# Gram products for two samples at a time in every tile of a DLRM tower, with the lookups and layers moved between the gram parts

## The chip, the cores and the metric

The kernel runs on one core of one Trainium2 chip. The metric is the device time of one execution in microseconds. All arithmetic is fp32, the lookup products are fp32r.

## What is computed

For 2048 samples, 32 embedding rows of 256 numbers are gathered from 32 tables. All 496 dot products between pairs of the 32 rows are taken, 16 context numbers are added, and three dense layers follow.

```
e = stack([tbl_f[ids[:, f]] for f in range(32)], axis=1)      # [2048, 32, 256]
dots = einsum('bnd,bmd->bnm', e, e)                            # per sample 32 x 32
z = dots[:, iu, ju]                                            # 496 pairs i < j
h = concatenate([z, dense_ctx], axis=1)                        # 512 features
h = maximum(h @ W_top1 + b_top1, 0)                            # 512
h = maximum(h @ W_top2 + b_top2, 0)                            # 256
y = h @ W_top3                                                 # 1
```

## The kernel before, in words

The samples are cut into 16 tiles of 128. Each engine has its own program, written out by hand, and the engines are tied by semaphores alone; nothing is reordered.

**Where rows come from.** Six of the 32 tables have 1000 rows and stay in SBUF. Their rows are looked up by TensorE (`look_up`, L326 to 342: a one-hot matrix made by VectorE in `make_one_hot` times the table, 32 matmuls for two tiles of samples at once, kept by ScalarE in `keep_looked_up`). Three lookups fall on each tile, two in tile 0. The other 26 fields are gathered by GpSimd with one indirect DMA per field and tile (`gather`, L288 to 297): 128 rows of 1 KB. Fields go in units of two, 13 units a tile, and there are 9 places (`PLACES`) for units that have landed; a gather waits until the unit nine before it has been turned (`turn_done`).

**Turning.** `turn` (L311 to 324) transposes a unit on TensorE, four transposes into one PSUM bank of a ring of `RING` = 4, and ScalarE or VectorE copies it into `turned` (`keep_turned`, L477 and L603); `ACT_UNITS` says which engine takes which unit. The copy of a tile's units must wait until the gram products of the tile before are done, since `turned` is a single buffer. Turn n waits for the copy of turn n - `RING`.

**Gram products.** `gram` (L344 to 362) goes over 32 groups in `PARTS` = 8 parts. In tiles 0 to 14 each sample has its own 32-column product, 128x32 weights and 31 moving columns, four samples side by side on four column tiles, into two banks (`gram_ps`). Each fp32 matmul stands in the trace twice, so one tile has 512 weight loads and 512 matmuls. The last tile alone uses `last_gram` (L364 to 380): two samples share the weights (64 columns) and the moving operand (62 columns), 256 weight loads and 256 matmuls, into four banks (`quad_ps`). Half of what they compute is between different samples and not used; ScalarE and VectorE first move the used blocks of the second samples to where `unfold` reads them (`align`).

**After the gram.** VectorE transposes the blocks of 32 (`unfold`), ScalarE picks the 496 pairs (`pick`), TensorE turns the features (`turn_features`), ScalarE keeps them, then come `layer1` (four parts, 32 matmuls in the trace), `keep_hidden1` on ScalarE, `layer2` (8 matmuls in the trace) and `last_layers` on VectorE.

**TensorE's order** around the change, for a tile t from 1 to 14: `turn_all` (the units of t not yet turned, the features of tile t - 1 after unit 6, then all of layer 1 of tile t - 1), and then eight times a slice of the tile's lookups (10 or 11 matmuls) and a gram part; layer 2 of t - 1 behind part 0; one unit of tile t + 1 is turned behind each of parts 3 to 6 (`EARLY_AFTER`), and a last slice of the lookups stands behind part 7.

ScalarE in tile t: three copies, the last lookup's copy, the pick, a copy, the features, a copy, `place` (the looked up rows into `turned`, two activations), two copies, `keep_hidden1`, then the lookups' copies. VectorE: `unfold`, six copies, then the one-hots with `last_layers` behind the first.

Of the kernel before, what the change touches and what calls it, by code (L numbers as in the profile page):

```python
# [38 lines left out]
def dlrm_tower(nc, dense_ctx, ids, small_ids, tables, w1, b1, w2, b2, w3, out):  # L39
# [30 lines left out]
    ACT_UNITS = [0, 1, 2, 6, 8, 10, 12]  # L70
    RING = 4
# [5 lines left out]
    EARLY_AFTER = [3, 4, 5, 6]  # L77

    TURN_FEATURES_AFTER = 6
    PARTS = 8  # L80
    GPP = GROUPS // PARTS
    BANK_GROUPS = GROUPS // 2
# [3 lines left out]
    LAST_BANKS = 4  # L86
    LAST_GROUPS = GROUPS // LAST_BANKS

# [22 lines left out]
    with ctx:  # L111
# [16 lines left out]
        with nc.sbuf_tensor("landed", [SP, SMALL, SUB, 2, D], fp32) as landed:  # L128
# [29 lines left out]
        last_h2 = turn_ps[2]  # L158
# [8 lines left out]
                   for bank in (gram_ps[:, 1, :], top_ps)]  # L167
# [24 lines left out]
        gram_done = sem("gram_done")  # L192

        last_gram_done = sem("last_gram_done")
# [115 lines left out]
        def _(pe):  # L310
# [33 lines left out]
            def gram(t, portion):  # L344
# [6 lines left out]
                if t == 0 and portion == PARTS // 2:  # L351
# [12 lines left out]
            def last_gram(portion):  # L364
                t = TILES - 1
                if portion == 0:
                    pe.wait_ge(act_kept, n_act_kept(BEGIN[t + 1] - 1))
                    pe.wait_ge(dve_kept, n_dve_kept(BEGIN[t + 1] - 1))
                    pe.wait_ge(placed, 2 * t + 1)
                    pe.wait_ge(unfolded, t)  # L370
                for g in range(portion * GPP, (portion + 1) * GPP):
                    at = g % LAST_GROUPS * WIDE
                    for c in range(CHUNKS):
                        for h in range(HALVES):
                            s = QUADS * g + 2 * h
                            pair = turned[:, c, s:s + 2, :]
                            last = pe.matmul(quad_ps[h * 2 * FIELDS:(h + 1) * 2 * FIELDS, g // LAST_GROUPS, at:at + WIDE],  # L377
                                             pair.rearrange("d s f -> d (s f)"), pair[:, :, 0:COLS], start=(c == 0), stop=(c == CHUNKS - 1))
                if (portion + 1) * GPP % LAST_GROUPS == 0:
                    last.then_inc(last_gram_done, 1)  # L380
# [48 lines left out]
            def turn_all(t):  # L429
# [5 lines left out]
                for m in range(M1):  # L435
                    layer1(t - 1, m)

            def look_between(t, k):

                made = FIRST[t + 1] - FIRST[t]  # L440
                for n in range(made):
                    begin, end = (n * (PARTS + 1) + made - 1) // made, ((n + 1) * (PARTS + 1) + made - 1) // made
                    if begin <= k < end:
                        look_up(FIRST[t] + n, PRODUCTS * (k - begin) // (end - begin),
                                PRODUCTS * (k + 1 - begin) // (end - begin))
# [291 lines left out]
```

## Time and profile before

| | |
|---|---|
| median of 3 runs | 896.95 us (895.36 to 898.39) |
| the profiled execution's own time | 892.55 us |
| its span in the profile | 890.7 us |
| TensorE matmul busy | 601.0 us (67%) |
| TensorE weight load busy | 524.1 us (59%) |
| VectorE busy | 225.9 us (25%) |
| ScalarE busy | 204.6 us (23%) |
| GpSimd busy | 398.0 us (45%) |
| mean granted TensorE clock | 0.85 |

A tile after the first takes 54.6 us. Busy shares are averages over stretches with different limits, so a tile is best read in stretches.

### The profile page before, as it was taken

Reading aid. Unit: us, or ns where it says so; the run is one execution under the profiler, and the core shown is the slowest. Engines: PE = TensorE matmul, PEld = TensorE weight load, DVE = VectorE, ACT = ScalarE, POOL = GpSimd, SP = SyncE. Lnnn points to the kernel's source line nnn. Section 1 sums busy time; section 2 is a strip of 40 time slices with the busy share of each in tenths; the row PEclk is TensorE's granted clock in tenths of the full one; section 3 lists DMA queues with packets and bytes.
Section 4 is the critical chain, followed back from the end, with each engine's and each line's share of the span. In section 5 each row is a group of like instructions: output and inputs, shape, how many; then the busy total and the mean of one; then the engine's idle time right before and its main releaser. Section 6 shows DMA issues by size and latency. Waiting matters only on the chain.

```text
span 890.7 us, 24184 instructions
## 1 busy us (share of the span) xinstructions
PE 601.0 (67%) x11019; PEld 524.1 (59%) x11019; DVE 225.9 (25%) x578; ACT 204.6 (23%) x369; POOL 398.0 (45%) x426
## 2 busy tenths in 40 slices
PE   3557668486684867748577584875848668486687
PEld 2456557375572756737467474765737657375586
DVE  3444313123130231402223032231312313123122
ACT  4252303103030030401313022130210303103042
POOL 7563625526255361543715347262462625526220
PEclk9688969698796987969789697896969969698799
DMA  9962312313122141321313224131231312313110
GB/s 220 243 204 68 99 42 77 94 44 102 43 78 83 50 107 38 83 73 56 108 37 87 63 57 118 32 96 49 70 105 39 101 41 76 88 41 90 43 38 2
DMA packets 37459, 70.97 MB, mean 80 GB/s; under 512 B 10382, under 2 KB 23438, under 8 KB 37358
## 3 DMA queue, kind: packets, MB, share of 16 engines
q0 software_dynamic: 20112, 54.95, 22.1%
q1 hardware_dynamic: 17246, 14.48, 7.0%
q8 instruction: 87, 1.43, 0.7%
q14 instruction: 14, 0.11, 0.0%
HBM read 69.39 MB, written 0.01 MB: 78 GB/s over the span
## 4 chain that ended last, share of the span: by engine, by line
PE 42%; another core or an unknown queue 30%; issue 13%; ACT 12%; DMA 1%; DVE 1%; POOL 1%; ACTq 0%; DVEq 0%
PE look_ps L338 18%; PE quad_ps L358 12%; PE top_ps L420 6%; ACT turned L501 4%; ACT turned L483 3%; PE turn_ps L322 3%; PE quad_ps L322 2%; ACT area L550 2%; ACT ahead L490 1%; DMA rows<-in_tbl,row_ids 1%; PE quad_ps L377 1%; POOL rows L295 1%; PE top_ps L407 1%; ACT products L506 0%
## 5 line engine op out<-in xcount | busy, mean ns | idle before, releaser
L295 POOL DMA_INDIRECT rows<-in_tbl,row_ids x419 | 397.2, 948 | 458.1 <-PE turn_ps L322 184.1
L338 PE MATMUL look_ps<-one_hot,small 125*128 125x256 f32 (+1 forms) x1536 | 251.9, 303 | 104.7 <-issue 92.8
L338 PEld LDWEIGHTS look_ps<-one_hot,small 125*128 125x128 f32 x1536 | 214.0, 202 | 116.6 <-issue 112.3
L358 PE MATMUL quad_ps<-turned 128*32 128x31 f32 x7680 | 140.0, 204 | 121.8 <-issue 121.5
L358 PEld LDWEIGHTS quad_ps<-turned 128*32 128x32 f32 x7680 | 108.8, 115 | 166.9 <-issue 153.3
L674 DVE TENSOR_SCALAR one_hot<-ids_across,sub_row 125x256 fp32r<-125x256 int32 (+1 forms) x384 | 112.0, 364 | 145.8 <-PE look_ps L338 126.6
L322 PE MATMUL turn_ps<-ident,rows 128*128 128x128 f32 x424 | 64.5, 282 | 28.5 <-issue 14.7
L655 DVE TENSOR_TENSOR top_ps<-top_ps,b_sb 128x256 f32<-128x256 f32 x15 | 6.5, 433 | 299.8 <-PE top_ps L420 299.8
L490 ACT ACTIVATE ahead<-look_ps 128x512 f32<-128x512 f32 (+1 forms) x48 | 28.3, 590 | 232.5 <-PE look_ps L338 219.1
L407 PE MATMUL top_ps<-area,w_sb 128*128 128x128 f32 x488 | 61.9, 276 | 19.5 <-issue 18.8
L550 ACT ACTIVATE area<-top_ps,b_sb 128x128 f32<-128x128 f32 x61 | 17.5, 368 | 227.5 <-remote 225.2
L407 PEld LDWEIGHTS top_ps<-area,w_sb 128*128 128x128 f32 x488 | 57.8, 192 | 18.1 <-issue 17.2
L322 PEld LDWEIGHTS turn_ps<-ident,rows 128*128 128x128 f32 x424 | 48.2, 143 | 31.8 <-issue 28.2
L483 ACT ACTIVATE turned<-turn_ps 128x512 f32<-128x512 f32 x57 | 35.0, 631 | 114.2 <-PE quad_ps L358 76.2
L322 PE MATMUL quad_ps<-ident,rows 128*128 128x128 f32 x414 | 60.1, 279 | 0.8 <-DMA rows<-in_tbl,row_ids 0.8
L483 ACT ACTIVATE turned<-quad_ps 128x512 f32<-128x512 f32 x55 | 33.9, 631 | 90.6 <-PE quad_ps L358 70.8
L420 PE MATMUL top_ps<-w_sb,area 128*128 128x256 f32 x120 | 49.4, 585 | 4.1 <-ACT area L550 4.1
L618 DVE STREAM_TRANSPOSE products<-quad_ps 128x992 f32<-128x992 f32 x15 | 18.3, 1217 | 127.7 <-PE quad_ps L358 127.7
L322 PEld LDWEIGHTS quad_ps<-ident,rows 128*128 128x128 f32 x414 | 46.5, 142 | 2.9 <-DMA rows<-in_tbl,row_ids 1.2
L501 ACT ACTIVATE turned<-ahead 128x768 f32<-128x768 f32 x31 | 45.0, 1552 | 0.0
L420 PEld LDWEIGHTS top_ps<-w_sb,area 128*128 128x128 f32 x120 | 35.6, 311 | 13.9 <-ACT area L550 6.1
L609 DVE COPY turned<-quad_ps 128x512 f32<-128x512 f32 (+1 forms) x49 | 33.0, 681 | 34.1 <-PE quad_ps L322 14.6
(50 smaller groups left out, 169.9 us busy)
## 6 DMA issues: line engine op xcount, KB each, us to landing
rows<-in_tbl,row_ids POOLq DMA_INDIRECT x419
ids_across<-in_small_ids SPq DMA_DIRECT2D x45, 128.0 KB
landed<-in_tbl SPq DMA_DIRECT2D x6, 896.0 KB
w_sb<-in_W_top SPq DMA_DIRECT2D x4, 256.0 KB
landed<-in_tbl SPq DMA_DIRECT2D x6, 104.0 KB
w_sb<-in_W_top SPq DMA_DIRECT2D x1, 512.0 KB
area<-in_dense_ctx SPq DMA_DIRECT2D x16, 8.0 KB
row_ids<-in_ids SPq DMA_DIRECT2D x1, 240.0 KB
```

The source lines that it names most:

```text
L295: pool.indirect_dma_start(out=rows[:, n % PLACES, j, :], out_offset=None, in_=tables[f], in_offset=bass.IndirectOffsetOnAxis(ap=row_ids[:, ...
L322: last = pe.transpose(turn_ps[n % RING][:, at:at + P], rows[:, n % PLACES, j, c * P:(c + 1) * P], ident[:, :])
L338: last = pe.matmul(look_ps[:, c * width:(c + 1) * width], small[:, f, r, part, c * P:(c + 1) * P], one_hot[n % 2][:, r, 0:width], start=(r ...
L358: last = pe.matmul(gram_ps[q * FIELDS:(q + 1) * FIELDS, g // BANK_GROUPS, at:at + COLS], turned[:, c, s, :], turned[:, c, s, 0:COLS], star ...
L407: last = pe.matmul(bank[:, m * P:(m + 1) * P], w1_sb[:, c, m * P:(m + 1) * P], features_t[:, c, :], start=(c == 0), stop=(c == KC - 1))
L420: last = pe.matmul((last_h2 if t == TILES - 1 else top_ps)[:, 0:HIDDEN2], hidden1[:, c, :], w2_sb[:, c, :], start=(c == 0), stop=(c == M1 ...
L483: act.activation(turned[:, :, :, f:f + len(unit)], turn_ps[n % RING][:, 0:CHUNKS * len(unit) * P].rearrange("p (c f s) -> p c s f", c=CHUN ...
L490: act.activation(ahead[:, f, :, 0:tiles * P], look_ps[:, 0:CHUNKS * tiles * P].rearrange("p (c s) -> p c s", c=CHUNKS), ACT.Copy).then_inc ...
L501: act.activation(turned[:, :, :, fs].rearrange("p c s f -> p f c s"), ahead[:, fs, :, half * P:(half + 1) * P], ACT.Copy).then_inc(placed, 1)
L550: act.activation(hidden1[:, m, :], bank[:, m * P:(m + 1) * P], ACT.Relu, bias=b1_sb[:, m:m + 1]).then_inc(h1_kept, 1)
L609: dve.tensor_copy(turned[:, :, :, f:f + len(unit)], turn_ps[n % RING][:, 0:CHUNKS * len(unit) * P].rearrange("p (c f s) -> p c s f", c=CHU ...
L674: last = dve.tensor_scalar(one_hot[n % 2][:, r, 0:width], ids_across[0:SP, n % IDS_RING, 0:width], sub_row[:, r:r + 1], None, ALU.is_equal)
```

## The change

- `gram` takes the form that `last_gram` had, in all tiles: 16 wide products a part (32 weight loads and 32 matmuls a part in the trace, 256 a tile), into four banks of their own. The semaphore `gram_banks` counts banks, each after two parts.
- PSUM has eight banks, so the ring of turned units shrinks from 4 to 2. `ACT_UNITS` becomes every even unit.
- `align` runs in all tiles: ScalarE for banks 0 and 2, VectorE for banks 1 and 3, and `unfold` waits for all of it.
- Two units instead of four are turned early, behind parts 5 and 6.
- The lookups are no longer cut in slices: each of parts 0, 1 and 2 has one whole lookup (32 matmuls) in front, and none stands behind part 7.
- Layer 1 of the tile before leaves `turn_all` (except in the last tile); its four parts stand behind gram parts 2 to 5, and layer 2 behind part 6. ScalarE's `keep_hidden1` moves behind `align(t, 2)`, VectorE's `last_layers` behind the one-hots.
- The ids of every tile are laid out on the host in the order that only the last tile had.

```diff
-    ACT_UNITS = [0, 1, 2, 6, 8, 10, 12]
-    RING = 4
+    ACT_UNITS = [0, 2, 4, 6, 8, 10, 12]
+    RING = 2
-    EARLY_AFTER = [3, 4, 5, 6]
+    EARLY_AFTER = [5, 6]
+    LAYER1_BEHIND = 2
+    LAYER2_BEHIND = 6
...
-        quad_ps = psum("quad_ps", [P, LAST_BANKS, 512])
-        gram_ps = quad_ps[:, 0:2, :]
-        turn_ps = [psum(f"turn_ps{i}", [P, 512]) for i in range(RING - 2)] + [quad_ps[:, b, :] for b in (2, 3)]
+        gram_ps = psum("gram_ps", [P, GRAM_BANKS, 512])
+        turn_ps = [psum(f"turn_ps{i}", [P, 512]) for i in range(RING)]
...
                 for g in range(portion * GPP, (portion + 1) * GPP):
-                    at = g % BANK_GROUPS * COLS
-                    for c in range(CHUNKS):
-                        for q in range(QUADS):
-                            s = q * FIELDS + g
-                            last = pe.matmul(gram_ps[q * FIELDS:(q + 1) * FIELDS, g // BANK_GROUPS, at:at + COLS],
-                                             turned[:, c, s, :], turned[:, c, s, 0:COLS],
-                                             start=(c == 0), stop=(c == CHUNKS - 1))
-                if portion == PARTS - 1:
-                    last.then_inc(gram_done, 1)
+                    at = g % BANK_GROUPS * WIDE
                     for c in range(CHUNKS):
                         for h in range(HALVES):
                             s = QUADS * g + 2 * h
                             pair = turned[:, c, s:s + 2, :]
+                            last = pe.matmul(gram_ps[h * 2 * FIELDS:(h + 1) * 2 * FIELDS, g // BANK_GROUPS, at:at + WIDE],
+                                             pair.rearrange("d s f -> d (s f)"), pair[:, :, 0:COLS],
+                                             start=(c == 0), stop=(c == CHUNKS - 1))
+                if (portion + 1) * GPP % BANK_GROUPS == 0:
+                    last.then_inc(gram_banks, 1)
...
-                for m in range(M1):
-                    layer1(t - 1, m)
+                if t == TILES - 1:
+                    for m in range(M1):
+                        layer1(t - 1, m)
             def look_between(t, k):
+                if k < FIRST[t + 1] - FIRST[t]:
+                    look_up(FIRST[t] + k, 0, PRODUCTS)
...
                 for k in range(PARTS):
                     look_between(t, k)
-                    if t < TILES - 1:
-                        gram(t, k)
-                    else:
-                        last_gram(k)
-                    if t > 0 and k == 0:
+                    gram(t, k)
+                    if 0 < t < TILES - 1 and LAYER1_BEHIND <= k < LAYER1_BEHIND + M1:
+                        layer1(t - 1, k - LAYER1_BEHIND)
+                    if t > 0 and k == (0 if t == TILES - 1 else LAYER2_BEHIND):
                         layer2(t - 1)
                     if k in EARLY_AFTER and t + 1 < TILES:
                         turn(BEGIN[t + 1] + EARLY_AFTER.index(k))
-                look_between(t, PARTS)
...
             def unfold(t):
-                dve.wait_ge(gram_done, t + 1)
+                dve.wait_ge(act_aligned, 4 * (t + 1))
+                dve.wait_ge(dve_aligned, 4 * (t + 1))
```

## Rows read from the trace of the kernel before

**Rows 1.** The page's groups of instructions, GpSimd's gathers.

```profile
L295 POOL DMA_INDIRECT rows<-in_tbl,row_ids x419 | 397.2, 948 | 458.1 <-PE turn_ps L322 184.1
```

**Rows 2.** Busy time in five stretches of one tile (start:end, length, busy us, count).

```profile
core 0: us, PE busy (x) PEld busy (x) DVE busy (x) ACT busy (x) POOL busy (x), PEclk, DMA share, GB/s
422.68:431.38 8.70, 8.31 (x74) 8.00 (x73) 5.31 (x12) 7.69 (x14) 5.89 (x7) 1.00 0.33 93
431.38:449.01 17.63, 4.34 (x19) 3.08 (x18) 1.10 (x4) 0.03 (x1) 11.14 (x12) 0.63 0.38 104
449.01:453.34 4.33, 4.01 (x64) 3.32 (x64) 0.00 (x0) 1.14 (x4) 0.00 (x0) 0.52 0.01 4
453.34:460.98 7.64, 7.55 (x234) 6.96 (x233) 3.06 (x11) 0.60 (x1) 0.00 (x0) 1.00 0.03 8
460.98:477.26 16.28, 12.64 (x320) 11.06 (x320) 3.54 (x10) 1.75 (x4) 7.69 (x8) 1.00 0.28 73
```

**Rows 3.** Timeline of that tile, from the first gather in turn_all to layer 2.

```profile
423.66 0.94 POOL L295 DMA_INDIRECT rows<-in_tbl,row_ids  x1 [3.01 <-PE turn_ps L322]
...
444.93 0.95 POOL L295 DMA_INDIRECT rows<-in_tbl,row_ids  x1 [0.30 <-issue]
...
449.01 1.01 PE L358 MATMUL quad_ps<-turned 128*32 128x31 f32 x57 [1.19 <-issue]
...
449.14 1.14 ACT L550 ACTIVATE area<-top_ps,b_sb 128x128 f32<-128x128 f32 x4 [17.74 <-remote]
...
450.34 3.38 PE L420 MATMUL top_ps<-w_sb,area 128*128 128x256 f32 x8 [0.31 <-ACT area L550]
```

**Rows 4.** Groups of instructions on GpSimd between 423.6 and 449.0 us.

```profile
L295 POOL DMA_INDIRECT rows<-in_tbl,row_ids x18 | 17.0, 946 | 8.2 <-issue 5.2 <-PE turn_ps L322 3.0
```

**Rows 5.** Timeline around one pair of gathers behind an early turn.

```profile
460.98 0.95 POOL L295 DMA_INDIRECT rows<-in_tbl,row_ids  x1 [15.11 <-PE quad_ps L322]
...
461.95 0.58 PE L358 MATMUL quad_ps<-turned 128*32 128x31 f32 x43
...
463.72 0.37 PE L358 MATMUL quad_ps<-turned 128*32 128x31 f32 x16 [0.45 <-issue]
```

**Rows 6.** Timeline of gram parts and lookup slices with no gather about.

```profile
454.95 0.76 PE L358 MATMUL quad_ps<-turned 128*32 128x31 f32 x64
...
455.65 1.58 PE L338 MATMUL look_ps<-one_hot,small 125*128 125x256 f32 x11
...
457.15 0.76 PE L358 MATMUL quad_ps<-turned 128*32 128x31 f32 x64
```

**Rows 7.** Timeline of the last tile, which has no gathers left.

```profile
858.90 0.42 PEld L322 LDWEIGHTS turn_ps<-ident,rows 128*128 128x128 f32 x4
...
863.80 3.74 PE L407 MATMUL top_ps<-area,w_sb 128*128 128x128 f32 x32
...
867.47 1.15 PE L377 MATMUL quad_ps<-turned 128*64 128x62 f32 x32
...
868.77 1.99 PE L420 MATMUL top_ps<-w_sb,area 128*128 128x256 f32 x8 [0.15 <-ACT area L550]
...
870.70 6.75 PE L377 MATMUL quad_ps<-turned 128*64 128x62 f32 x224
```

**Rows 8.** Timeline of VectorE and ScalarE where a gram ends, in two tiles.

```profile
421.48 1.22 DVE L618 STREAM_TRANSPOSE products<-quad_ps 128x992 f32<-128x992 f32 x1 [7.66 <-PE quad_ps L358]
421.53 0.64 ACT L483 ACTIVATE turned<-turn_ps 128x512 f32<-128x512 f32 x1 [9.53 <-PE quad_ps L358]
...
871.89 0.72 ACT L522 ACTIVATE quad_ps<-quad_ps 32x248 f32<-32x248 f32 x2 [3.17 <-PE quad_ps L377]
...
877.49 0.89 DVE L626 COPY quad_ps<-quad_ps 32x248 f32<-32x248 f32 x2 [2.84 <-PE quad_ps L377]
```

**Rows 9.** Timeline near the start: a lookup, and a turn under gathers.

```profile
18.88 5.94 PE L338 MATMUL look_ps<-one_hot,small 125*128 125x256 f32 x32 [0.93 <-issue]
...
34.23 0.37 PE L322 MATMUL turn_ps<-ident,rows 128*128 128x128 f32 x1 [1.04 <-issue]
```

More of the change, by code:

```diff
@@ L157, in dlrm_tower @@
         last_h1 = [top_ps, look_ps, turn_ps[0], turn_ps[1]]
-        last_h2 = turn_ps[2]
+        last_h2 = gram_ps[:, 0, :]
         spare_ps = turn_ps[0]
@@ L166, in dlrm_tower @@
         high_ps = [bank[0:SP, 0:AT_ONCE * D].rearrange("p (r d) -> p r d", r=AT_ONCE)
-                   for bank in (gram_ps[:, 1, :], top_ps)]
+                   for bank in (gram_ps[:, GRAM_BANKS - 1, :], top_ps)]
         square = products[:, 0:COLS * ZROW].rearrange("p (i j) -> p i j", j=ZROW)
@@ L350, in gram @@
                         pe.wait_ge(unfolded, t)
[L351 removed]
+                if t == 0 and portion * GPP == GROUPS - BANK_GROUPS:
                     pe.wait_ge(low_parts, SMALL * STEPS)
                 for g in range(portion * GPP, (portion + 1) * GPP):
[L354 to L372 removed]
+                    at = g % BANK_GROUPS * WIDE
                     for c in range(CHUNKS):
@@ L376, in last_gram @@
                             pair = turned[:, c, s:s + 2, :]
[L377 to L380, printed above, removed]
+                            last = pe.matmul(gram_ps[h * 2 * FIELDS:(h + 1) * 2 * FIELDS, g // BANK_GROUPS, at:at + WIDE],
[3 more added lines that the diff above has]
+                    last.then_inc(gram_banks, 1)
             def turn_features(t):
@@ L514, in pick, with align @@
                 act.activation(features[:, CYCLIC:PAIRS], diagonal[:, 0:HALF, HALF], ACT.Copy).then_inc(picked, 1)
-            def align(b):
-                act.wait_ge(last_gram_done, b + 1)
-                both = quad_ps[:, b, 0:LAST_GROUPS * WIDE].rearrange("p (g h j) -> p h g j", h=2, j=COLS)
+            def align(t, b):
+                act.wait_ge(gram_banks, GRAM_BANKS * t + b + 1)
+                both = gram_ps[:, b, 0:BANK_GROUPS * WIDE].rearrange("p (g h j) -> p h g j", h=2, j=COLS)
                 for q in (1, 3):
@@ L577, in _ @@
                 if t > 0:
-                    for i in ACT_UNITS[:3]:
+                    for i in ACT_UNITS[:2]:
                         keep_turned(BEGIN[t] + i)
@@ L582, in _ @@
                         keep_looked_up(FIRST[t] - 1)
+                    keep_turned(BEGIN[t] + ACT_UNITS[2])
                     pick(t - 1)
@@ L589, in _ @@
                         keep_turned(BEGIN[t] + i)
-                    keep_hidden1(t - 1)
+                    if t == TILES - 1:
+                        keep_hidden1(t - 1)
                 for n in range(FIRST[t], FIRST[t + 1] - 1):
                     keep_looked_up(n)
-            align(0)
-            align(2)
+                align(t, 0)
+                align(t, 2)
+                if 0 < t < TILES - 1:
+                    keep_hidden1(t - 1)
             last_pick()
@@ L699, in _ @@
                 for k, n in enumerate(range(FIRST[t] + 1, FIRST[t + 1] + 1)):
+                    if n == FIRST[t + 1]:
+                        align(t, 1)
                     if n < len(LOOKUPS):
                         make_one_hot(n)
-                    if k == 0 and t > 0:
-                        last_layers(t - 1)
+                if t > 0:
+                    last_layers(t - 1)
                 if t == TILES - 1:
-                    last_layers(t - 1)
-            align(1)
-            align(3)
-            last_unfold()
+                    align(t, 1)
+                align(t, 3)
+            unfold(TILES - 1)
             last_pick()
```

38 lines of the change are left out of this document (12 added, 26 removed).

## The prediction

> **What bounds the kernel now.** The page comes first: no engine is busy all the time, TensorE least idle, GpSimd with its 419 gathers of 948 ns not the bound [rows 1]. So a tile has to be read in stretches [rows 2], the tile that starts at 422.68 and is followed by the next at 477.26, 54.58 us. TensorE is busy for 8.31 of 8.70 us while it turns units, then for 4.34 of 17.63 us, in which 19 matmuls start, then for nearly all of 12 us (4.33 and 7.64), and then for 12.64 of 16.28. The reader is to see that 13.3 us of idle time lie in one stretch. What it waits for there is told by the timeline [rows 3]: nothing that the profile shows ("issue"), and ScalarE, which needs the last matmul of layer 1, is let go at 449.14, at the moment at which TensorE runs again and 57 matmuls start in one microsecond. What else goes on is the gathers: the first at 423.66, the last issued at 444.93, 18 of them back to back [rows 3, 4]. 449.01 less 423.66 is 25.35 us, or **1.41 us a gather**, more than the 1.25 us at which GpSimd issues them. The same length stands around a pair of gathers behind an early turn: from 460.98 to 463.72 is 2.74 us, 1.37 a gather, and TensorE makes 43 matmuls in it and then stands [rows 5]. With no gather about it does not stand: gram part, slice and gram part follow each other at 454.95, 455.65 and 457.15 [rows 6]. And in the last tile, where no gathers are left, the gram starts at 867.47, 8.57 us after the first turn at 858.90 [rows 7], where the tile above took over 26. I read this as one cause: while gathers are being carried out, at about 1.4 us each, TensorE's matmuls complete only in a trickle, and it can run ahead of them by a limited count. Between 422.68 and 449.01, 26.3 us, 74 and 19 matmuls started, 93 in all [rows 2]. What fits into such a stretch is thus a number of matmuls, not an amount of time.
>
> **The change, part by part.** Durations are those of the profiled execution, 892.55 us, 4.40 us under the median of the runs.
>
> Gram. A narrow part of 64 matmuls takes 0.70 us (454.95 to 455.65), 10.9 ns each [rows 6], so 5.6 us a tile. The wide form takes 6.75 us for 224, 30.1 ns each [rows 7], so 7.7 us for 256. In TensorE's own time the change costs 2.1 us a tile, though it halves the instructions. A rule speaks for the change here: the Trainium skill (TensorE: Matmul & The Clock Gate, the section on 56 against 53.3 ns) says that starts of matmuls are never closer than some 25 ns however few the columns. By it the narrow gram would cost 12.8 us and the wide one save 5.1; the row shows less than half of that floor, and the sum goes by the row.
>
> Gathers and ring. A tile has 26 gathers either way. Before, 4 units were turned early, so 8 gathers ran beside gram parts, and 18 made the long stretch. Now 2 are turned early, so 4 gathers run beside parts and 11 units, **22 gathers**, follow in one stretch: 22 x 1.41 = 31.0 us, and with the 0.98 us from first turn to first gather (422.68 to 423.66) 32.0 us, against 26.3.
>
> What fills that stretch. Eleven turns come first. With a ring of 2 each turn waits for the copy of the turn two before, and so for its own kind's completion. How fast turns complete under gathers no row shows alone: the bounds are a turn per gather (1.41 us) and one per pair of gathers (2.8 us, then the gathers set the pace of the turns). I take 1.41, since in the first 8.70 us the turns and all of layer 1 started without a stop [rows 2]: 11 turns and the features, some 17 us. In the 15 us left stands the first lookup, 32 matmuls. The 93 matmuls that started in 26.3 us, scaled to 32.0, are 113; turns and features take 48, the lookup 32, and the other 33 are the first gram part, 32. The second lookup must wait for the first to complete and be copied, so it comes after the stretch.
>
> After the stretch. A slice of 11 lookups takes 1.50 us [rows 6], so a lookup of 32 takes 4.4. Second lookup 4.4, with 1.0 more for the lowered clock at its start: at 0.52 of the granted clock layer 2 took 3.38 us [rows 2, 3] and in the last tile 1.99 [rows 7], and a whole lookup near the start, at the lower of the two levels, 5.94 [rows 9]. A rest of part 0: 0.3. Gram part 1: 1.0. Third lookup 4.4. Parts 2 to 6: 4.8. Layer 1 in four parts: 3.7 [rows 7]. Two early turns: 0.9. Wait for `keep_hidden1` (1.14 us [rows 3], partly beside part 6): 0.5. Layer 2 at full clock: 2.0. Then the second early turn sends two gathers, and part 7's last semaphore completes only behind them: 3.0, of which the part's 1.0 is hidden. ScalarE's copy, now with no lookup slice in front of the next turn: 0.75 [rows 8]. The sum is 26.75, against 28.25 before (449.01 to 477.26). Gained in it are 11 of 85 lookup matmuls each 1.50 us that move forward (2.9), the stops beside four pairs of gathers (16.28 less 12.64 and what lies in them, some 4), and 1.4 of layer 2; lost are layer 1, wide parts and the waits.
>
> `align` (0.72 us on ScalarE, 0.89 on VectorE for a pair [rows 8]) is hidden for banks 0 to 2 by later parts. Bank 3 lies in front of `unfold` (1.22 us), so VectorE's first copy comes 0.9 us later; turns are paced by gathers there, which hides it, and without that cover it costs 0.9 a tile. One-hots have the wait for the third lookup's slot ahead of them, hidden by parts 1 and 2. `last_layers` and the dense load of SP have a whole turn phase to spare. The host's order of ids costs the chip nothing.
>
> A tile then takes 32.0 + 26.75 = 58.7 us, 4.1 more. Tiles 1 to 14 make 57. Last tile: the copies in a ring of 2 (0.43 turn, 0.64 copy and the ways between, about 0.8 a unit) and layer 1 still in `turn_all` bring the gram from 8.6 to about 13 us behind the first turn: 4.4. Start: a ring of 2 in 15 turns beside the splitting of tables, and the first gram wide: 2, between -1 and 6. Together 57 + 4.4 + 2 = 64 over 892.55 is 956.5, and with the 4.4 to the median **961, given as 960**.
>
> **The rivals.**
>
> A, turns go at the pace of a pair of gathers. Near the start single turns did start as far apart as the 34.23 row shows, alone after 1.04 us of idle time [rows 9]. Then nothing but turns fits into the stretch, and the first lookup and part 0 fall behind it: 5 us a tile more, 70 in all, about 1030. Against it: the table loads were under way there.
>
> B, the completions go on at turn speed through the whole stretch. Then the second lookup fits too: 5.4 us a tile less than the sum, 76 in all, about 885. For it: the first 8.70 us of the stretch in rows 2, with 74 matmuls. Against it: the rest of it, where 19 started in 17.63 us.
>
> C, on the other side, faster: the stall belongs to TensorE's own instructions and the gathers only go along with it. Its place is the 13.3 us of the long stretch and the 3.6 of the last one in rows 2. Of 711 matmuls a tile (74, 19, 64, 234 and 320) 256 go, so 0.64 are left, and of 16.9 us of idle time 6.1 go; the wide gram gives back 2.1, the copy and the alignment 0.9 more: 3.1 a tile gained, 43, and with the 6.4 of both ends 37 less: about 860. It decides if the stop ends earlier than 1.4 us times the gathers. For it: stops in rows 5 fall inside the dense narrow part, which is where instructions come fastest. Against it: rows 6 and 7 have the same density and no stop, and the stretch's length is the gathers' to some hundredths.
>
> D, a limit for each start of a matmul, whatever its columns, that rows 6 hide. If a narrow product cost what a wide one does, 30.1 ns [rows 7], the narrow gram would take 15.4 us and the wide one gain 7.7 where the sum loses 2.1: 9.8 a tile, 137 in all, about 825. Against it: 64 in 0.70 us. The Trainium skill's page named above has the milder form of this rule; by it the time would be about 860.
>
> E, the change does nothing: what TensorE gains and loses is all absorbed by the gathers' 26 x 1.41 = 37 us a tile. About 897.
>
> **Chances.** The forecast with its bounds (925 to 985) has 0.45, A 0.12, B 0.13, C 0.24, D 0.02, E 0.04. Differences under 0.3% can't be told from none. B is split, 0.08 faster, 0.02 the same and 0.03 slower. Faster: 0.34; the same: 0.06; slower: 0.60. Most of the chance is on two sides, so the likeliest case's own range is 925 to 985; the range given reaches to C's price and leaves out A: 855 to 1000.
>
> **What would show it.** Right: one long stretch of 22 gathers a tile and a stop that ends 31 us behind the first; one lookup and no more in it; no stop in the gram parts behind single pairs, except ahead of the next turns; wide parts of 0.96 us; about 450 matmuls a tile. Wrong: a stop that ends before 1.4 us times its gathers (C), two lookups inside it (B), or turns 2.5 us and more apart (A). The forecast falls if the stretch between two tiles' first turns is under 55 us.

## The result, and the profile after

The kernel after takes **984.99 us** (median of 4 runs, 981.01 to 989.16), the kernel before, measured beside it, 896.15 us (4 runs, 894.34 to 898.39). The ratio is 1.099 with a 95% interval of 1.093 to 1.105: slower, as forecast (960, range 855 to 1000), and 25 us above the forecast number. The profiled execution took 987.82 us with a span of 986.0. Executions of one kernel on one chip lie within 1.5% of each other, but for the kernel after on a chip of the experiments, where the profiled one took 698.84 us at a mean granted TensorE clock of 0.94 and the other 674.95 us at 0.97; the faster one is compared there.

The page of the kernel after, groups of instructions:

```profile
L294 POOL DMA_INDIRECT rows<-in_tbl,row_ids x419 | 397.2, 948 | 552.0 <-PE turn_ps L321 410.2
L321 PE MATMUL turn_ps<-ident,rows 128*128 128x128 f32 x838 | 167.1, 348 | 204.4 <-issue 76.8
L337 PE MATMUL look_ps<-one_hot,small 125*128 125x256 f32 (+1 forms) x1536 | 260.0, 336 | 63.0 <-issue 57.1
L358 PE MATMUL gram_ps<-turned 128*64 128x62 f32 x4096 | 166.5, 236 | 27.4 <-issue 25.1
```

The gathers are the same 419 of 948 ns [rows 1], and GpSimd waits 94 us longer between them: it is not the bound. The turns (the transposes of gathered rows on TensorE) now have 204.4 us of idle time in front of them. As before, the tile has to be read in stretches. Busy time of the kernel after in the two stretches of one tile, from its first turn to the end of the stop (the time in which TensorE hardly starts a matmul) and from there to the next tile's first turn:

```profile
core 0: us, PE busy (x) PEld busy (x) DVE busy (x) ACT busy (x) POOL busy (x), PEclk, DMA share, GB/s
457.75:490.39 32.64, 17.00 (x90) 14.21 (x90) 7.73 (x16) 8.63 (x14) 20.82 (x22) 0.71 0.35 96
490.39:518.90 28.51, 25.65 (x359) 23.81 (x360) 6.76 (x23) 4.32 (x11) 3.78 (x4) 0.92 0.09 26
```

The first stretch answers to the first two of [rows 2] and is 6.3 us longer, the second to the last three and is 0.3 us longer. This tile took 61.2 us; the first 13 of the 15 steps between the unfolds of neighbouring tiles have a mean of 60.2 (54.6 before). Inside the tile, TensorE and GpSimd in the timeline of the kernel after, with one of VectorE's copies:

```profile
459.11 0.94 POOL L294 DMA_INDIRECT rows<-in_tbl,row_ids  x1 [2.80 <-PE turn_ps L321]
...
466.99 0.63 PE L321 MATMUL turn_ps<-ident,rows 128*128 128x128 f32 x4 [1.61 <-DVE turned L590]
...
469.09 0.63 PE L321 MATMUL turn_ps<-ident,rows 128*128 128x128 f32 x4 [1.47 <-issue]
...
472.62 0.69 DVE L590 COPY turned<-turn_ps 128x512 f32<-128x512 f32 x1 [5.79 <-remote]
...
473.46 1.09 PE L321 MATMUL turn_ps<-ident,rows 128*128 128x128 f32 x4 [3.75 <-DVE turned L590]
...
477.64 1.09 PE L321 MATMUL turn_ps<-ident,rows 128*128 128x128 f32 x4 [3.09 <-issue]
...
478.38 4.64 PE L337 MATMUL look_ps<-one_hot,small 125*128 125x256 f32 x26
...
487.93 0.95 POOL L294 DMA_INDIRECT rows<-in_tbl,row_ids  x1 [0.30 <-issue]
...
490.39 1.54 PE L358 MATMUL gram_ps<-turned 128*64 128x62 f32 x23 [0.45 <-issue]
...
491.86 5.44 PE L337 MATMUL look_ps<-one_hot,small 125*128 125x256 f32 x32
...
498.32 4.09 PE L337 MATMUL look_ps<-one_hot,small 125*128 125x256 f32 x32
...
514.89 1.15 PE L358 MATMUL gram_ps<-turned 128*64 128x62 f32 x32
...
518.90 1.08 PE L321 MATMUL turn_ps<-ident,rows 128*128 128x128 f32 x4 [2.87 <-ACT turned L460]
```

From the first gather of the stretch (459.11) to the end of the stop (490.39) are 31.3 us for 22 gathers, 1.42 each (1.41 in [rows 3]). The last three turns start 4 us apart. That it is the completion of a matmul that comes late shows at the turn of 466.99: VectorE, idle for 5.79 us, begins its copy at 472.62 only, and the turn of 473.46 had to wait for that copy. One lookup and 9 matmuls of part 0 fit in, 23 of part 0 do not. At the end of the tile the next turn waits 2.87 us for ScalarE's copy. I read this as part 7's completion, held back by the pair of gathers of 515.23 and 516.48, which the copy has to wait for.

Two places outside the ordinary tile cost more. The last step but one between unfolds (tile 14) took 67.6 us against 54.0 in the kernel before. Its timeline in the kernel after:

```profile
917.02 1.98 PE L358 MATMUL gram_ps<-turned 128*64 128x62 f32 x32
918.92 7.09 PE L337 MATMUL look_ps<-one_hot,small 125*128 125x128 f32 x32
...
945.09 0.70 PE L321 MATMUL turn_ps<-ident,rows 128*128 128x128 f32 x4 [2.84 <-ACT turned L460]
...
961.17 1.15 PE L358 MATMUL gram_ps<-turned 128*64 128x62 f32 x32
```

Busy time and granted clock in that place of the kernel after:

```profile
917.00:925.00 8.00, 8.00 (x62) 7.87 (x61) 0.00 (x0) 1.08 (x3) 0.00 (x0) 0.50 0.00 0
```

The granted clock was 0.50, with TensorE busy for all 8 us: a part takes 1.98 us instead of 1.08, a lookup of half the columns 7.09. And the last tile needs 16.1 us from its first turn (945.09) to the gram (961.17), against 8.57 [rows 7]. The account of the 95.3 us between the two profiled executions (987.82 and 892.55), by the starts of the unfolds: 0.7 up to the first, 13 x 5.6 = 73, tile 14 13.6, last tile 6.1, end 1.6.

### The profile page after: what moved, and what is told of

It reads as the page before. It is cut to its first block and busy times, and to the rows that moved or that the text cites. A ratio compares the mean times of both kernels' runs of the same rounds, so it can differ in the third digit from the quotient of the medians.

```text
span 986.0 us, 16627 instructions
## 1 busy us (share of the span) xinstructions
PE 686.2 (70%) x7179; PEld 615.1 (62%) x7179; DVE 248.5 (25%) x638; ACT 229.9 (23%) x429; POOL 398.0 (40%) x426
## 5 line engine op out<-in xcount | busy, mean ns | idle before, releaser
L321 PE MATMUL turn_ps<-ident,rows 128*128 128x128 f32 x838 | 167.1, 348 | 204.4 <-issue 76.8
L337 PEld LDWEIGHTS look_ps<-one_hot,small 125*128 125x128 f32 x1536 | 246.1, 244 | 68.6 <-issue 66.6
L321 PEld LDWEIGHTS turn_ps<-ident,rows 128*128 128x128 f32 x838 | 126.0, 180 | 235.3 <-issue 232.5
L358 PE MATMUL gram_ps<-turned 128*64 128x62 f32 x4096 | 166.5, 236 | 27.4 <-issue 25.1
L358 PEld LDWEIGHTS gram_ps<-turned 128*64 128x64 f32 x4096 | 146.0, 148 | 51.7 <-issue 38.6
L460 ACT ACTIVATE turned<-turn_ps 128x512 f32<-128x512 f32 x112 | 68.6, 613 | 388.9 <-remote 261.8
L590 DVE COPY turned<-turn_ps 128x512 f32<-128x512 f32 x98 | 67.5, 688 | 259.5 <-remote 129.1
L608 DVE COPY gram_ps<-gram_ps 32x248 f32<-32x248 f32 x64 | 27.5, 430 | 240.3 <-PE gram_ps L358 200.0
L499 ACT ACTIVATE gram_ps<-gram_ps 32x248 f32<-32x248 f32 x64 | 22.1, 346 | 181.6 <-PE gram_ps L358 180.9
L402 PE MATMUL top_ps<-w_sb,area 128*128 128x256 f32 x120 | 29.9, 392 | 0.2 <-ACT area L527 0.2
L402 PEld LDWEIGHTS top_ps<-w_sb,area 128*128 128x128 f32 x120 | 21.6, 189 | 3.5 <-ACT area L527 0.3
```

Of the source, the lines that this page charges most:

```text
L321: last = pe.transpose(turn_ps[n % RING][:, at:at + P], rows[:, n % PLACES, j, c * P:(c + 1) * P], ident[:, :])
L337: last = pe.matmul(look_ps[:, c * width:(c + 1) * width], small[:, f, r, part, c * P:(c + 1) * P], one_hot[n % 2][:, r, 0:width], start=(r ...
L358: last = pe.matmul(gram_ps[h * 2 * FIELDS:(h + 1) * 2 * FIELDS, g // BANK_GROUPS, at:at + WIDE], pair.rearrange("d s f -> d (s f)"), pair[ ...
L402: last = pe.matmul((last_h2 if t == TILES - 1 else top_ps)[:, 0:HIDDEN2], hidden1[:, c, :], w2_sb[:, c, :], start=(c == 0), stop=(c == M1 ...
L460: act.activation(turned[:, :, :, f:f + len(unit)], turn_ps[n % RING][:, 0:CHUNKS * len(unit) * P].rearrange("p (c f s) -> p c s f", c=CHUN ...
L590: dve.tensor_copy(turned[:, :, :, f:f + len(unit)], turn_ps[n % RING][:, 0:CHUNKS * len(unit) * P].rearrange("p (c f s) -> p c s f", c=CHU ...
```

## The experiments

The main theory was that of the prediction: **TensorE's completions are held back while a gather is carried out**, 1.41 us for each. Its rival was C, that the stall belongs to TensorE's own instructions. A second question was which part of the change costs what. Twelve programs, two of them the kernels unchanged, ran in four sets on four chips. The time of a tile below is the step from one unfold's start to the next (L618 of the kernel before).

**Gathers left out.** In both kernels, only the first tile is gathered:

```diff
-            for n in range(len(UNITS)):
+            for n in range(BEGIN[1]):
                 gather(n)
```

(`n_gathered` counts accordingly.) For the kernel before:

> The kernel before with the gathers of tiles 1 to 15 left out (their units are turned from rows that tile 0 gathered). Theory 1 (matmuls complete only in a trickle while gathers are carried out, 1.4 us each): the long stop and the four short ones go, a tile takes the sum of TensorE's own work, about 31 us (8.7 us of turns and layer 1, 96 lookup matmuls in 13.1, gram 5.6, layer 2 2.0, early turns 1.7), the whole about 563 us. Rival C (the stops belong to TensorE's own instructions): stops of the same order stay, above 800 us.

For the kernel after:

> The changed kernel with the gathers of tiles 1 to 15 left out. Theory 1: a tile takes the work without stops, about 42 us: a turn phase of some 12 us, set by the ring of 2 and the copies as in its last tile, lookups 13.1, wide parts of 1.08 us each 8.6, layer 1 4.3, layer 2 and two turns 2.9, waits 1 to 2; the whole about 730 us. So the change would cost TensorE's side itself some 11 us a tile, more than the 5.6 a tile seen with gathers. Rival C: stops stay, above 880 us.

Measured: 533.61 and 699.72 us, with 30.5 and 41.0 us a tile. But the kernel before itself, as it is, took **561.68 us** on that chip (3 runs, 560.62 to 564.71), not 896. The runs could not decide between the theories: on this chip there was no stop to take away. Most of what before_nogather took less than the 563 us expected lies at the start: the first unfold came at 72.0 us, against 93.9 on the first chip. The two runs did show that the change costs more, not less, where no gathers are about: 10.5 us a tile.

**Early turns and buffers.** In the kernel before, first the early turns alone:

```diff
-    EARLY_AFTER = [3, 4, 5, 6]
+    EARLY_AFTER = [5, 6]
```

> The kernel before with two early turns a tile in place of four, behind parts 5 and 6; nothing else. Theory 1: the long stretch grows from 18 to 22 gathers, 5.6 us; two short stops of 1.4 us and two turns of 0.43 go from the rest; some 1.9 us a tile more, about 920 us. Rival (early turns don't matter, ring and wide gram do): 893 to 900 us. Rival C: no gather counts, the same time as before.

then with the ring as well:

```diff
-    ACT_UNITS = [0, 1, 2, 6, 8, 10, 12]
-    RING = 4
+    ACT_UNITS = [0, 2, 4, 6, 8, 10, 12]
+    RING = 2
...
-        turn_ps = [psum(f"turn_ps{i}", [P, 512]) for i in range(RING - 2)] + [quad_ps[:, b, :] for b in (2, 3)]
+        turn_ps = [psum(f"turn_ps{i}", [P, 512]) for i in range(RING)]
```

> The kernel before with the ring of 2, ScalarE taking every even unit, and two early turns; narrow gram, lookups in slices and layer 1 as before. Theory 1 (the long stretch of 22 gathers hides the slower turns): 925 to 940 us, nearly all of it from the two early turns. Rival (the ring is a cost of its own: turns that wait for each other's late completion push layer 1 and lookups out of the stretch): 960 us or more.

Measured on the same chip: 601.61 us (599.30 and 603.92), ratio 1.070 [1.056, 1.084], and 628.46 us (623.81 and 633.11), ratio 1.118 [1.096, 1.140]. The figures expected were for a chip with stops and can't be compared; the order, ring 2 above early turns alone, came out. With two early turns the waits of TensorE for gathered rows came to 34.3 + 19.3 us (21.6 + 11.6 in the run of the kernel before that follows); with the ring of 2 the wait for copies took their place. The waits of TensorE with the ring of 2 (us in total, times, longest):

```profile
PE turn_ps L322 <- DVE turned L609: 28.4, 60, 2.9
PE turn_ps L322 <- ACT turned L483: 21.8, 18, 1.4
PE turn_ps L322 <- DMA rows<-in_tbl,row_ids: 15.4, 3, 11.4
```

**The kernel before again, unchanged, for its profile** on another chip:

> The kernel before, unchanged, for its profile on the chip of these runs. Two kinds of chip have shown themselves: one on which the kernel before takes 896 us and TensorE stands still while gathers are carried out (Rows 3), and one on which it takes 562 us. If this run is near 560 us: no gap in TensorE of more than 3 us beside the gathers of a tile, tiles of about 33 us, and TensorE's clock near 0.98. If it is near 896 us: the gap of 17 us in each tile as in Rows 3. The theory that the stop belongs to the gathers and to nothing in the program expects the first kind wherever the total is near 560.

It took 562.47 us. Its gathers on the page, as a group of instructions and as a DMA queue (packets, MB, share of 16 engines), and then the busy time of one tile:

```profile
L295 POOL DMA_INDIRECT rows<-in_tbl,row_ids x419 | 397.2, 948 | 132.7 <-issue 117.9
q0 software_dynamic: 20112, 54.95, 35.2%
```

```profile
299.90:331.10 31.20, 30.75 (x705) 28.59 (x705) 13.38 (x34) 11.16 (x21) 23.64 (x25) 1.00 0.43 121
```

The gathers are the same count and length for GpSimd as in [rows 1], yet it now issues them one after another, and TensorE beside 25 of them is busy for 30.75 of 31.20 us. The DMA engines don't work any faster here either: 35.2% of 560.7 us is 197 us of each engine for the gathers, and on the chip of the first measurement the page had 22.1% of 890.7 us, 197 us too:

```profile
q0 software_dynamic: 20112, 54.95, 22.1%
```

So the stop is neither more work for the DMA engines nor slower issue on GpSimd. One chip has it and another has not.

**The kernel after again, unchanged,** beside it:

> The kernel after, unchanged. On a chip that stops under gathers 985 us, ratio 1.10. On one that does not, the version without later gathers took 699.7 us against 533.6 us for the same version of before; with the gathers put back (before gained 28 us with them: 561.7 - 533.6) about 700 + 15 = 715 us, range 700 to 730, ratio 1.27. There a tile takes 41 to 42 us. If the stops under gathers were the main price of the change, the ratio here would instead be near 1.05 or below.

Two runs, 674.95 and 698.84 us, where 700 to 730 were expected, so 1.20 times before by the faster and 1.24 by the other: the change costs this chip more than the 1.10 it costs where stops are. In the profiled one, 698.84 us, tiles take 40.9 us. The granted clocks, 0.941 of 697.0 us and 0.972 of 673.1 us, mean 82 and 38 us at the lower of the two levels, half of full speed; 44 us more of it can make 22 of the 24 us between the two, an estimate. What lowered the clock is open.

**The gram and the buffers without the new order.** The kernel after, with the lookups in slices, layer 1 in `turn_all` and layer 2 behind part 0 again:

```diff
-                if k < FIRST[t + 1] - FIRST[t]:
-                    look_up(FIRST[t] + k, 0, PRODUCTS)
+                made = FIRST[t + 1] - FIRST[t]
+                for n in range(made):
...
-                    if 0 < t < TILES - 1 and LAYER1_BEHIND <= k < LAYER1_BEHIND + M1:
-                        layer1(t - 1, k - LAYER1_BEHIND)
-                    if t > 0 and k == (0 if t == TILES - 1 else LAYER2_BEHIND):
+                    if t > 0 and k == 0:
                         layer2(t - 1)
...
+                look_between(t, PARTS)
```

> The gram of the change (two samples in a product), with its two buffers of turns and its two early turns, but the order of before: the lookups in slices, layer 1 in the turn phase, layer 2 behind the first gram part. On a chip without stops: the version of before with two buffers and two early turns took 623.8 us; the wide gram adds 2.1 us a tile by my sum for TensorE's columns, x16 = 34 us, so 658 us if only the gram counts beside the buffers, and 700 or more if the clock falls with it; if the order of the change is what costs, this version is much below the kernel after. On a chip with stops: 900 + 34 + 20 = 950 us.

Measured: 652.91 us (652.83 and 653.00), ratio 1.161 [1.154, 1.168], near the 658 expected if the gram alone counts beside the buffers. A tile takes 38.0 us.

**The new order alone,** in the kernel before:

```diff
+                if k < FIRST[t + 1] - FIRST[t]:
+                    look_up(FIRST[t] + k, 0, PRODUCTS)
...
+                    if 0 < t < TILES - 1 and 2 <= k < 2 + M1:
+                        layer1(t - 1, k - 2)
+                    if t > 0 and k == (0 if t == TILES - 1 else 6):
                         layer2(t - 1)
```

> The order of the change alone: the gram of before, its four buffers and four early turns, with a whole lookup in front of each of the first three gram parts, layer 1 behind the third to sixth and layer 2 behind the seventh. The same products in the same tile, so on a chip without stops within 1% of before (562 us, range 556 to 570) if order is free; 20 us or more above it if order is what makes the change slow. On a chip with stops 880 to 900 us: the first lookup of a tile then lies whole in the stop.

Measured: 584.11 us (583.68 and 584.54), ratio 1.038 [1.032, 1.045]: order is not free. One place where it shows is the wait of the first turn for ScalarE's copy, which the last slice behind part 7 had covered; such waits come to 14.9 us in 13 places. TensorE with the new order, then in the kernel before on the same chip:

```profile
279.66 0.63 PE L322 MATMUL turn_ps<-ident,rows 128*128 128x128 f32 x4 [1.16 <-ACT turned L481]
```

```profile
330.99 1.58 PE L338 MATMUL look_ps<-one_hot,small 125*128 125x256 f32 x11
332.42 0.60 PE L322 MATMUL quad_ps<-ident,rows 128*128 128x128 f32 x4
```

On chips without stops (before took 561.68 us on the one and 563.17 on the other, so sums may cross them) the bill is then, by medians and with the spread of the runs in brackets: early turns 40 us (38 to 42), the ring 27 (20 to 34), the wide gram with its alignment 24 (20 to 29), the new order 22 by the faster run of the kernel after (46 by the other); in all 112 (136). Added in this order, no part of the change gains there. Of the versions that do the whole work none was faster than the kernel before; those with a part of the change alone ran only on chips without stops.

**Three kinds of tiles in one program.** To have stops and no stops side by side whichever chip came up, tiles 5 to 8 fetch half of the rows and tiles 10 to 13 none:

```diff
+                some = P // 2 if t in HALF_ROWS else P
-                        out=rows[:, n % PLACES, j, :], out_offset=None, in_=tables[f],
+                        out=rows[0:some, n % PLACES, j, :], out_offset=None, in_=tables[f],
...
+                if UNITS[n][0] not in NO_GATHERS:
                     gather(n)
```

> The kernel before with three kinds of tiles in one program: the gathers of tiles 5 to 8 fetch 64 of 128 rows each, those of tiles 10 to 13 are left out, the others are whole. Read by the periods between the unfolds of consecutive tiles. If TensorE's stops belong to gathers, then on a chip that has stops (896 us for the kernel before) whole tiles take 54.6 us, tiles without gathers 31 us, and tiles with half of the rows 54.6 us if a stop is for each instruction, 41 to 43 us if it goes by rows. If the stops belong to TensorE's own instructions, all tiles take 54.6 us there. On a chip without stops (562 us) whole tiles take 31 to 34 us, tiles without gathers 30.5 us, and half tiles lie between; a gather of half the rows keeps GpSimd for 0.95 us if that time is for the instruction, for half of it if it goes by rows.

> The same three kinds of tiles in the kernel after. On a chip with stops: whole tiles 60.2 us, tiles without gathers 41 us if the stops are gathers' (then the change costs 10 us a tile where no gather is about, 5.6 us where they are, because the stop covers part of it), 60 us if they are not. On a chip without stops: 41 us in all three kinds, since TensorE and the copies of turned rows bound the tile and gathers do not.

A third chip without stops came up (before: 566.29 us), so what half the rows do to a stop was not measured. The two took 553.36 and 698.71 us. Gathers run ahead of their tile, so a tile's time goes with the gathers of the next. Of the kernel before, steps with whole gathers took 31.3 to 31.5 us (31.9 the last), with half rows 31.4 to 31.8 (35.1 the first, as the same step of the kernel before unchanged, 35.2) and with none 30.5; a gather of half the rows kept GpSimd for 900 ns, so its time is almost all for the instruction. Tiles of the kernel after took 41.0 us in all three kinds: on a chip without stops gathers do not bound it at all.

**Four groups of tiles, on a chip with stops.** The last two kernels cut the order in its two halves and leave out the gathers of one tile in each group ("whole lookups" stand in front of parts 0 to 2; "late layers" are layers 1 and 2 behind the gram parts):

```diff
+    WHOLE, LATE, NO_GATHERS = [5, 6, 7, 11, 12, 13], [8, 9, 10, 11, 12, 13], [4, 7, 10, 13]
...
+                if t in WHOLE:
+                    if k < made:
+                        look_up(FIRST[t] + k, 0, PRODUCTS)
+                    return
...
+                    if t in LATE and 2 <= k < 2 + M1:
+                        layer1(t - 1, k - 2)
+                    if t > 0 and k == (6 if t in LATE else 0):
                         layer2(t - 1)
```

> The kernel before with its tiles in four groups, read by the periods between unfolds: tiles 1 to 4 as they are, 5 to 7 with whole lookups in front of the first three gram parts, 8 to 10 with the layers behind the gram parts, 11 to 13 with both (the order of the change); the gathers of the last tile of each group (4, 7, 10, 13) are left out. On a chip without stops: 31 to 32 us, then whichever group takes 33 to 34 us holds the cost of the order (33.7 with both, as measured). I expect it in the whole lookups (33 us, since no slice is left behind the last gram part to cover the wait for the copy of the next turn) and 32 us in the layers alone. On a chip with stops: 54.6 us in all whole tiles and 31 to 34 in the tiles without gathers, if the stops are gathers'.

> The same four groups for the wide gram: tiles 1 to 4 with slices and early layers (38.0 us measured on a chip without stops), 5 to 7 whole lookups (expected 40 us: 1.5 us for a first lookup at the lower clock behind the turn phase, 0.85 us for the uncovered wait behind the last part), 8 to 10 late layers alone (38.5 us), 11 to 13 both, the kernel after (41.0 us measured). No gathers in tiles 4, 7, 10 and 13. On a chip with stops: about 60 us in whole tiles, 38 to 41 us in those without gathers.

This chip took 895.54 us for the kernel before, as the first one had. The two ran in 846.60 and 874.57 us. Busy time by tiles, narrow gram (kernel before with groups): plain without gathers, plain, whole lookups, whole lookups without gathers, both halves of the order, both without gathers:

```profile
203.30:233.80 30.50, 30.03 (x705) 28.14 (x705) 12.52 (x34) 11.11 (x21) 0.00 (x0) 1.00 0.10 18
234.00:288.60 54.60, 37.11 (x705) 32.33 (x705) 12.68 (x35) 11.08 (x21) 24.77 (x26) 0.84 0.25 71
288.60:348.80 60.20, 41.75 (x715) 36.19 (x715) 12.66 (x34) 11.18 (x21) 24.64 (x26) 0.76 0.24 65
348.80:384.30 35.50, 32.01 (x704) 30.15 (x704) 12.57 (x35) 11.18 (x21) 0.00 (x0) 0.93 0.06 16
593.80:658.50 64.70, 43.15 (x715) 37.18 (x715) 12.88 (x34) 11.28 (x21) 24.64 (x26) 0.79 0.22 60
658.50:690.90 32.40, 30.49 (x704) 28.14 (x704) 12.43 (x35) 11.22 (x21) 0.00 (x0) 1.00 0.07 18
```

The first two lines decide between the theories. They are neighbours in one program on one chip, with the same 705 matmuls in the same order: without gathers 30.5 us, with 26 of them 54.6. The 30.5 is to the tenth what a tile without gathers took on the two chips without stops. **The long stops are the gathers'**, and C has fallen as their cause: TensorE's own stream of short instructions runs through in 30.03 us of busy time.

A small stop of C's kind does exist, though. The tile with whole lookups and without gathers (the fourth line, GpSimd busy 0.00) has two, 1.38 and 1.09 us long, in narrow parts that follow each other with at most a turn, four matmuls, between them:

```profile
376.73 0.44 PE L360 MATMUL quad_ps<-turned 128*32 128x31 f32 x27
378.54 0.53 PE L360 MATMUL quad_ps<-turned 128*32 128x31 f32 x37 [1.38 <-issue]
```

The last gather before them was issued at 346.97, over 29 us earlier. The other narrow tiles without gathers do not have them: the plain one has a lookup slice between any two parts, the one with both halves has a lookup, a quarter of layer 1, or layer 2 between any two. They are 2.5 of the 3.0 us that this tile takes more than the one with both halves (35.4 against 32.4 us). What causes them is open.

The same for the wide gram (kernel after with groups): slices with and without gathers, whole lookups, both halves with and without gathers:

```profile
153.70:212.10 58.40, 41.85 (x450) 37.25 (x450) 14.80 (x39) 12.90 (x25) 24.64 (x26) 0.82 0.25 67
212.10:250.90 38.80, 34.97 (x446) 31.90 (x445) 14.29 (x38) 12.84 (x25) 3.79 (x4) 0.96 0.10 26
304.90:365.20 60.30, 41.18 (x449) 37.01 (x449) 14.59 (x39) 12.76 (x25) 24.80 (x26) 0.83 0.23 63
613.90:675.00 61.10, 43.15 (x450) 38.83 (x451) 14.67 (x39) 12.90 (x25) 24.65 (x26) 0.78 0.25 63
675.00:716.10 41.10, 36.45 (x449) 33.22 (x448) 14.18 (x38) 12.81 (x25) 3.79 (x4) 0.92 0.09 24
```

(In the tiles called without gathers four are left, behind the early turns at the end.) All kinds of steps in one table; in brackets a step that follows a tile without gathers:

| us a tile, chip with stops | plain / slices | whole lookups | late layers | both |
|---|---|---|---|---|
| narrow, with gathers | 54.6 (54.7) | 60.3 (60.6) | 58.0 (58.8) | 64.7 (62.8) |
| narrow, without | 30.5 | 35.4 | 32.2 | 32.4 |
| wide, ring 2, 2 early, with gathers | 58.5 (54.0) | 60.2 (55.8) | 58.7 (56.4) | 61.0 (57.9) |
| wide, without | 38.8 | 39.7 | 38.2 | 41.2 |

Without gathers the whole change costs 41.2 - 30.5 = 10.7 us a tile; with them 60.2 - 54.6 = 5.6 in the kernels themselves. So 5.1 of 10.7 us are hidden in the stops. (The 41.2 is like the tiles of the longer execution of the kernel after. The shorter one was not profiled; its 24 us less, spread over 15 tiles, would be 1.6 us a tile, an estimate, so 10.7 may be high by that.) My reading is that what is hidden is above all the turns: they wait for copies while TensorE could not have gone on anyway. The turns of the tile without gathers, up to what follows them, take 12.4 us with the ring of 2 and 5.0 with the ring of 4, though two more units belong to the longer one. The kernel after with groups, then the kernel before with groups:

```profile
674.79 0.63 PE L323 MATMUL turn_ps<-ident,rows 128*128 128x128 f32 x4 [2.84 <-ACT turned L471]
...
687.21 4.08 PE L339 MATMUL look_ps<-one_hot,small 125*128 125x256 f32 x32
```

```profile
204.63 0.60 PE L324 MATMUL turn_ps<-ident,rows 128*128 128x128 f32 x4
...
209.60 3.74 PE L409 MATMUL top_ps<-area,w_sb 128*128 128x128 f32 x32
```

From the same table: gram, ring and early turns 3.9 us (58.5 - 54.6), the order 1.7 to 2.5 with the wide gram, but 8 to 10 with the narrow one. For the wide gram about 60 us were expected in every tile with gathers; 54.0 to 61.0 were measured. For the narrow one 54.6 were expected in all groups, since a gather was thought to set the tile whatever the order, and this failed: that the order would be dearer with the narrow gram than the whole change was not expected.

One reason why it is dearer there shows at a pair of gathers (637.66 and 638.91) beside a narrow part, in the kernel before with groups, tile with both halves:

```profile
637.31 0.61 PE L360 MATMUL quad_ps<-turned 128*32 128x31 f32 x46
638.22 0.28 PE L360 MATMUL quad_ps<-turned 128*32 128x31 f32 x6 [0.29 <-issue]
638.95 0.28 PE L360 MATMUL quad_ps<-turned 128*32 128x31 f32 x6 [0.46 <-issue]
639.70 0.28 PE L360 MATMUL quad_ps<-turned 128*32 128x31 f32 x6 [0.47 <-issue]
```

46 matmuls start at full pace, and then six at a time, every 0.7 us. A part of 64 takes 3.1 us instead of 0.7. Short matmuls run into this after half a microsecond; a part of 32 wide ones beside such a pair (514.89 above) starts whole in 1.15 us, its gathers at 515.23 and 516.48. In the plain order the part beside a pair stops too, but later and for fewer matmuls [rows 5], since the lookup slice in front of it, 11 long matmuls, takes up part of the gathers' time; how much of the difference this makes was not tested, and the small stops without gathers can add to it.

Tile 14's loss comes with the new order too, and only with the wide gram and its small ring. On the chips without stops tile 14 took 51.2 us in the kernel after, 38.6 with the wide gram in the old order and 32.5 with the narrow gram in the new order; on the chip with stops it took 58.3 with the wide gram in the old order, against 67.6. Lookups and layers were not told apart there. In the kernel after on a chip without stops:

```profile
620.00:630.00 10.00, 10.00 (x71) 9.77 (x71) 1.66 (x8) 0.38 (x1) 7.56 (x8) 0.50 0.37 107
```

## Why the prediction held

- **The cause** (gathers hold TensorE's completions, 1.41 us each): shown by the tiles without gathers, and by 22 gathers that make 31.3 us where 31.0 was forecast. True only of chips with stops; that there are others the prediction did not know, and that the kernel after was measured on a chip of the same kind as the kernel before was luck.
- **What fills the stretch** is the step that failed in part. It took the 93 matmuls of [rows 2] as a count that grows with time, 113 in 32 us, and 17 us for turns and features. It was 90 matmuls in 32.6 us, no more than the 93 of the shorter stretch before, and 20.6 us for turns and features (457.75 to 478.38): with a ring of 2 the last three turns wait for the copy of the one two before, 4 us apart, which is rival A at the end of the phase. So 23 matmuls of part 0 came behind the stop, 1.5 us instead of 0.3.
- **After the stretch** 26.75 us were forecast and 28.5 measured. The second lookup (5.4 against 4.4 + 1.0, its first 2.1 us at a granted clock of 0.50) and layer 2 (1.99 against 2.0) were right; one of the rows given for that 1.0 does not bear it, since in the profile the lookup of 18.88 [rows 9], 5.94 us long, has a granted clock of 1.00, not the lower level; the third was 4.0 instead of 4.4, parts 1.08 us each instead of 0.96, the wait behind the last pair 2.87 plus the part, 4.0 against 3.75. The tile came to 60.2 us instead of 58.7: with 5.6 instead of 4.1 a tile, 1.5 us in 13 tiles are some 20 us.
- **Gram +2.1 us a tile:** 8 parts of 1.08 us against 0.70 are 3.0. Without stops the wide gram cost 24 us in all (20 to 29), 1.5 a tile. The sign was right and the size near, between the two. The tile without gathers makes its narrow parts, 64 matmuls, in 0.69 to 0.76 us, so with no gather about a start costs 11 ns as in [rows 6]. The rule of the Trainium skill that the prediction weighed (TensorE: Matmul & The Clock Gate, some 25 ns between starts) does not hold for these, and going by the row was right.
- **Tile 14** was counted as any other and cost 8 us more than another; its granted clock was 0.65 on the mean (0.84 before) and 0.50 where it was shown. **The last tile** was put at 13 us and took 16.1, and gathers of its own (946.07 to 950.8) still ran beside its turns. **Start** 2 against 0.7.
- **The number:** between the profiled executions 64 us were forecast and 95 measured. 7 of the missing 31 came back by chance, since the profiled execution of the kernel before lay 4.4 us under its median and that of the kernel after 2.8 above its own. The 985 lies at the upper end of the likeliest case's own 925 to 985.
- **Rivals.** A held for the last three turns of eleven. B (a second lookup in the stretch) did not happen. C fell as the cause of the long stops with the tile without gathers (its small stops, 2.5 us, stood in narrow parts with at most a turn between them, which neither kernel has in tiles 1 to 14), and D with that tile's narrow parts. E, that all is absorbed, is half true: 5.1 of 10.7 us a tile are.

## What to carry to other kernels

When an engine stands still and nothing in the profile releases it, look for what else runs exactly as long, and take that away for single tiles of one program: neighbours in one trace decide what two programs on two chips can't. If TensorE is held back by gathers, what counts beside them is the number of its instructions (93 matmuls in 26.3 us before, 90 in 32.6 after), so my advice, not tested by itself, is to put long matmuls there and short ones elsewhere; and a change that costs time in every engine can look cheap, because the stop hides it. Work that stands last before a wait for a copy covers that wait: moving it costs what it covered.

## What was not expected of the hardware

- **The stops depend on the chip.** The same kernel took 561 to 566 us on three chips and 895.5 us on a fourth; by its time the chip of the first measurement (896) was of that kind. GpSimd's 948 ns a gather and the DMA engines' 197 us are the same on both. What differs is open. Whether a stop goes by the gather or by its rows is open too.
- Once TensorE is held beside gathers, its matmuls start in steps of 0.7 us or a multiple, mostly one to six at a time; two steps are the 1.41 us of a gather.
- TensorE also stopped twice, for 1.38 and 1.09 us, with no gather about, in narrow parts with next to nothing between them (376.73 above).
- TensorE's granted clock stayed at 0.50, the lower level, for 10 us of unbroken work (620 to 630 above) behind turns that waited for copies; lookups in slices did not bring this about in the same tile.
